# Two-row units at three places of the last stage of a conditioned bottleneck adapter, and one 512 KB store cut in two

## The reference

```python
# x [4,1024,512], h_lang = cond_256 [4,128]; DIM=512, BN=128, H=128, DELTA_SCALE=0.1
dWd = ((h_lang @ Wdd.T + bdd) * DELTA_SCALE).reshape(B, BN, D)     # Wdd: [65536, 128]
dWu = ((h_lang @ Wdu.T + bdu) * DELTA_SCALE).reshape(B, D, BN)     # Wdu: [65536, 128]
Wd_b = Wd + dWd
Wu_b = Wu + dWu
down = jax.nn.relu(jnp.einsum('bld,bnd->bln', x, Wd_b) + bd)
up = jnp.einsum('bln,bdn->bld', down, Wu_b) + bu
return x + up
```

## Time and profile before

| | |
|---|---|
| runs | 213.40, 213.16, 213.97 us (median 213.4) |
| profiled execution | 212.81 us, its span 210.9 us |
| bytes moved | 85.11 MB, 403 GB/s over the span; HBM read 76.55 MB, written 8.39 MB |
| DMA engines, busy share by slices of the span | 0.6 in the first, 0.7 in the last, 0.9 or more in the 38 between |
| PE, DVE, ACT, POOL busy | 168.1, 159.9, 57.5, 74.1 us |

### The profile page before, as it was taken

One profiled execution on the slowest core, in us unless ns is written; L12 is line 12 of the kernel. 1 busy time (PEld: TensorE's weight loads), 2 busy tenths in 40 slices (PEclk: granted clock), 3 DMA queues, 4 the chain that ended last, 5 costly groups with the idle time before them and its releaser, 6 DMA issues.

```text
span 210.9 us, 3068 instructions
## 1 busy us (share of the span) xinstructions
PE 168.1 (80%) x1146; PEld 99.2 (47%) x1146; DVE 159.9 (76%) x88; ACT 57.5 (27%) x102; POOL 74.1 (35%) x58
## 2 busy tenths in 40 slices
PE   1066399677777673999895999999999999998980
PEld 0011153313324140476663767568666665557960
DVE  2866999899999999944744877458859999992770
ACT  2001014111111201053542454454444434543000
POOL 2000000000000000035843857599586578797000
PEclk9999999797969699799999999999999999999996
DMA  6999999999999999999999999999999999999997
GB/s 226 423 384 399 423 419 416 426 421 423 423 423 423 423 423 423 423 421 421 418 423 419 418 419 418 421 418 423 423 418 418 410 401 415 419 385 386 344 344 241
DMA packets 19510, 85.11 MB, mean 403 GB/s; under 512 B 1573, under 2 KB 9769, under 8 KB 10282
## 3 DMA queue, kind: packets, MB, share of 16 engines
q1 hardware_dynamic: 19490, 84.94, 99.2%
q10 hardware_dynamic: 8, 0.00, 0.0%
HBM read 76.55 MB, written 8.39 MB: 403 GB/s over the span
## 4 chain that ended last, share of the span: by engine, by line
DMA 65%; DVE 18%; PE 11%; issue 2%; SPq 0%; DVEq 0%
DMA w<-in_L_cond_Wdu_dram 35%; DMA w<-in_L_cond_Wdd_dram 30%; DVE wt L299 18%; PE bank L634 8%; PE acc L527 2%; PE acc L644 1%; PE gt L553 0%; SPq L225 0%; DVE xs L341 0%; DVE down L331 0%; DVEq L340 0%
## 5 line engine op out<-in xcount | busy, mean ns | idle before, releaser
L299 DVE STREAM_TRANSPOSE wt<-w 128x2048 f32<-128x2048 f32 x63 | 145.5, 2311 | 36.5 <-DMA w<-in_L_cond_Wdu_dram 25.9
L527 PE MATMUL acc<-wt,st 128*32 128x512 f32 x496 | 72.0, 706 | 33.4 <-DVE wt L299 33.0
L477 POOL TENSOR_TENSOR xs<-xs,bu_all 128x1024 f32<-128x1024 f32 x16 | 37.9, 2368 | 109.1 <-PE bank L607 109.1
L527 PEld LDWEIGHTS acc<-wt,st 128*32 128x32 f32 x496 | 14.7, 120 | 73.8 <-DVE wt L299 38.0
L634 PE MATMUL bank<-wu_b,down 128*128 128x128 f32 (+1 forms) x192 | 30.9, 313 | 0.5 <-issue 0.5
L617 PE MATMUL dn<-xt,wd_b 128*128 128x256 f32 x128 | 30.6, 382 | 0.0
L634 PEld LDWEIGHTS bank<-wu_b,down 128*128 128x128 f32 x192 | 26.5, 191 | 6.6 <-issue 4.5
L484 POOL TENSOR_TENSOR xs<-up_s,xs 128x512 f32<-128x512 f32 x20 | 25.2, 1278 | 5.0 <-ACT up_s L430 4.9
L617 PEld LDWEIGHTS dn<-xt,wd_b 128*128 128x128 f32 x128 | 23.0, 190 | 3.4 <-issue 0.8
L372 ACT ACTIVATE g_rows<-acc 128x512 f32<-128x512 f32 x16 | 9.6, 597 | 50.2 <-PE acc L527 48.7
L413 ACT ACTIVATE xt<-bank 128x512 f32<-128x512 f32 x32 | 17.4, 595 | 11.9 <-PE bank L607 11.9
(11 more groups left out here) (32 smaller groups left out, 35.5 us busy)
## 6 DMA issues: line engine op xcount, KB each, us to landing
w<-in_L_cond_Wdd_dram SPq DMA_DIRECT2D x32, 1024.0 KB, 7.4
w<-in_L_cond_Wdu_dram SPq DMA_DIRECT2D x32, 1024.0 KB, 10.1
xs<-in_x_dram SPq DMA_DIRECT2D x8, 1024.0 KB, 12.3
out_dram<-xs SPq DMA_DIRECT2D x4, 1024.0 KB, 10.8
out_dram<-xs SPq DMA_DIRECT2D x7, 512.0 KB, 5.6
out_dram<-xs SPq DMA_DIRECT2D x2, 256.0 KB, 4.9
base_d<-in_L_cond_Wd_dram SPq DMA_DIRECT2D x1, 256.0 KB, 7.1
down<-in_L_cond_bdd_dram SPq DMA_DIRECT2D x1, 256.0 KB, 7.3
```

Of the source, the lines that this page charges most:

```text
L299: nc.vector.transpose(wt[:, tslot].rearrange("p r (k j) -> p k r j", j=QUAD), w[:, slot, :].rearrange("p (k r h) -> p k r h", r=R, h=QUAD) ...
L477: nc.gpsimd.tensor_tensor(xs[:, b, i0:i0 + UNIT_I], xs[:, b, i0:i0 + UNIT_I], bu_pair, ALU.add).then_inc(bu_added, 1)
L527: last = nc.tensor.matmul(a[TILE * place:TILE * (place + 1)], st[:, r, low * TILE:(low + 1) * TILE], wt[:, slot + h, r], start=low == 0 an ...
```

## The change

Three units of four rows by 128 columns become two of two rows each, or one of the two, at three places. The third quarter of batch 1's first four rows (unit 18) is cut in two: the first half stays between the last sums and the turn, the second half goes behind the turn. The last quarter of batch 0's first four rows (unit 20 before) is cut in two as well, and its store of 512 KB becomes two stores of 256 KB. There are 34 units then, of which POOL has 21, DVE 13. ACT's copy is as long as the unit.

```diff
-UNITS += [(b, i, 4, q * QD, QD) for q in range(2, 4) for b in range(EARLY) for i in range(0, I, 4)]
+UNITS += [(0, 0, 4, 2 * QD, QD), (0, 4, 4, 2 * QD, QD)]
+UNITS += [(1, 0, 2, 2 * QD, QD), (1, 2, 2, 2 * QD, QD), (1, 4, 4, 2 * QD, QD)]
+UNITS += [(0, 0, 2, 3 * QD, QD), (0, 2, 2, 3 * QD, QD), (0, 4, 4, 3 * QD, QD)]
+UNITS += [(1, 0, 4, 3 * QD, QD), (1, 4, 4, 3 * QD, QD)]
...
-POOL_UNITS = 20
+POOL_UNITS = 21
...
-STORES += [(b, slice(i, i + 4), slice(HALF, D)) for b in range(B) for i in range(0, I, 4)][:-1]
+STORES += [(0, slice(i, i + 2), slice(HALF, D)) for i in range(0, 4, 2)] + [(0, slice(4, I), slice(HALF, D))]
+STORES += [(b, slice(i, i + 4), slice(HALF, D)) for b in range(1, B) for i in range(0, I, 4)][:-1]
...
+        def unit_size(e):
+            _, rows, cols = unit_at(e)
+            return (rows.stop - rows.start) * (cols.stop - cols.start)
+
         def unit_sums(e, bank_or_copy):
             b, rows, cols = unit_at(e)
-            return bank_or_copy.rearrange("p (i d) -> p i d", d=cols.stop - cols.start)
+            return bank_or_copy[:, 0:unit_size(e)].rearrange("p (i d) -> p i d", d=cols.stop - cols.start)
...
-                nc.scalar.activation(up_s[:, e % UP_RING], bank_of("up", e)[:], ACT.Copy
+                size = unit_size(e)
+                nc.scalar.activation(up_s[:, e % UP_RING, 0:size], bank_of("up", e)[:, 0:size], ACT.Copy
                                      ).then_inc(up_copied, 1)
```

## The result

The changed kernel takes 212.0 us against 213.1 us, medians of 18 runs each; the ratio is 0.9945 with a 95% interval of 0.9927 to 0.9963, so 0.8 to 1.6 us less. 0.2 us less were forecast. The time lies under the range (212.6 to 213.9), and the gain is about five times the forecast one and just over the half per cent that was given a chance of 0.06. A second measurement of the same two kernels (12 and 28 runs) gave 0.9962 (0.9934 to 0.9990), so 0.8 us.

A forecast was written before the change was run, and what follows sets the result against it. The DMA engines were taken to bound the kernel. Filling their dry spot saves 0.2 us (0.25 less what is left) with nothing added, so 213.4 - 0.2 = 213.2 us; range 212.6 to 213.9.

The forecast's parts named there:

- What bounds the kernel: Whole kernel: the DMA engines bound it, one queue filling them for 99.2% of the span; PE and DVE add nothing at the end.
- Parts 1 and 2: Halved unit brings turn 0.1 us earlier; batch 0's last quarter, begun with two rows, issues first store 0.8 us earlier.
- Parts 3 and 4: Behind the fifth store: 730 KB against 595 needed, so no second dry spot; one store more costs DMA engines nothing.
- So 0.2 to 0.3 us is all that an earlier fifth store can give back: First second-half store: issued earlier, it regains only the dry spot's 75 to 113 KB, 0.21 to 0.32 us at 350 GB/s.
- the spot: DMA share falling to 0.91, then 0.70, from 195.9 to 197.0, until the fifth store flows; 75 to 113 KB missing.
- Smaller stores drain slower: Rival on store sizes: 0.28 us per store added, giving 213.7, or 213.5 with the dry spot filled; chance 0.12.
- The engine that ends last never ran dry: Rival at the end: an engine lagging about 1 us had work through the dry spot; no change, 213.4; chance 0.33.

## Why the prediction was wrong

**What bounds the kernel: right.** The DMA engines do, and PE's and DVE's last units have slack; 0.63 of the 0.7 us of the tail can be read from what the DMA engines wrote in it.

**Parts 1 and 2: right.** The turn came 0.12 us earlier (forecast 0.1), PE's last quarter started no later, the first store was issued 0.87 us earlier (forecast 0.8) and the second 0.45 behind it. DVE's half units take 0.87 us for two (forecast 0.4 each). Parts 3 and 4 of the prediction held too: no second dry spot came, and the added store cost nothing that a trace shows.

**"So 0.2 to 0.3 us is all that an earlier fifth store can give back": this step failed.** Its first half held: the spot was worth 0.10 MB, 0.30 us. The sentence behind it, "from 197.0 to 209.2 nothing else is missing", did not. I measured the spot against "the rate that follows (about 350)", as if that rate were given. It was in part a consequence of the spot. At the same distances from the last sums the change writes 371 and 356 GB/s where the kernel before writes 353 and 345, another 0.11 MB and 0.33 us, a term that the sum had at nothing. A warning stood in the rows: the rate ahead of the spot was 384, with a DMA share of 1.09 for 1.04 behind it. The engines looked nearly as busy behind the spot, and wrote 10% less.

**"Smaller stores drain slower": wrong.** I did see the step from 384 to 350 "exactly where the sizes change", and put it down to the sizes. It was exactly where the spot was, too. 512 KB pieces drain at 382 GB/s ahead of a spot, and 1 MB ones at 340 behind one. The fixed part of 2.0 us that this rival names beside its price is given by that section of the Trainium skill for DMAs issued from GpSimd; here SP issues them, and three further stores left the tail as it was.

**"The engine that ends last never ran dry": no trace shows it.** If it held, filling the spot would have given nothing, and the last packets would come as late as before. The tail is shorter by 0.7 us, and in windows of 0.25 us the last packets come until 21.3 us behind the start of the last sums before, and until 20.5 in the change.

**The numbers.** Forecast 213.2, measured 212.0. The medians of before agree (213.4 in three runs, 213.1 in eighteen), so this isn't the level. 0.7 us are in the tail of both pairs of traces; the rest of the 1.1 us of the first measurement is not shown by any trace, and within its interval and the second measurement's (0.8 us) nothing has to be looked for there. The prediction called itself wrong if the time moved by over 1 us, with two reasons: something outside the last 20 us, which no trace shows, or a drain rate that depends on how the stores are cut. The rate did change, but with the spot and not with the cut.

**What stays open** is why the engines drain slower behind a standstill, and why the rate also falls where there is none: from 384 to 371 and 356 in the change. The rate falls roughly with the depth of the spot: shares of 1.05, 0.96, 0.85, 0.78 and 0.36 at 7 to 8.1 us are followed by 356, 355, 345, 345 and 340 GB/s at 12 to 16 (0.86 in another kernel by 350). A possible reading is that 16 engines that start together on one store stay in step and get in each other's way, while those that were never idle are spread out over several stores. The packets in the profile carry no engine's number, so this is only argued and not shown.

## What to carry to other kernels

When all DMA engines run dry for a moment in front of a long stretch of stores, price the spot with what it does to the rate behind it, not only with the bytes missing in it. Here that doubled the price. Compare the rate ahead of it with the rate behind it, since the busy share shows less than half of the difference, and take this for an upper bound: about two fifths of it came back here. To keep a queue from running dry, cut the first piece of work behind the critical result small, so that its store is issued early, and don't merge the stores that follow.

## What was not expected of the hardware

The same 1 MB stores drain at 383 GB/s if they follow loads without a break, and at 340 GB/s behind about 2 us of standstill, and the stores behind them stay there to the end, 24 us later. The DMA share is 1.08 in the one and 1.03 to 1.05 in the other. A packet of 1 KB then takes 49 ns for 45, so that the share hides more than half of the loss. Behind a spot that is only partly dry (0.78 for 1.1 us) the rate is 353 and 345 GB/s, and 371 and 356 without it. No loss by size was seen: 512 KB and 1 MB stores ran at 382 and 383 GB/s ahead of any spot, and 256 KB ones at 364 where 512 KB ones ran at 356.
